# The 18 looped units of a Mamba and token-mixing kernel written out as straight code on every engine

## The reference

```
x = x + mamba(channel_norm(x))        # per batch a sequence of 2304 tokens of 128 channels, plus one token
t = to_tokens(x)                      # 576 tokens of 512 channels
t = t + route(token_norm(t))          # tokens 1..128 are replaced by a weighted sum of 8 of 256 memory blocks
out = from_tokens(t)

def mamba(seq):
    u, z = split(seq @ in_proj)                      # 256 inner channels
    u = silu(conv4(u) + bias)
    dt, B, C = split(u @ x_proj)                     # rank 8, 16 states, 16 states
    dt = softplus(dt @ dt_proj + bias)
    for each token:                                  # a scan over 2305 tokens
        h = exp(dt * A) * h + (dt * u) * B           # 16 states per inner channel
        y = sum(h * C)
    return (y + u * D) * silu(z) @ out_proj
```

## Time and profile before

| | |
|---|---|
| median of 3 runs | 1336.19 us (1335.76 to 1339.44) |
| the profiled execution | 1343.07 us, of which 1341.3 us span |
| VectorE busy | 1211.3 us, 90% |
| TensorE busy (matmul) | 1094.4 us, 82% |
| GpSimd busy | 1089.0 us, 81% |
| ScalarE busy | 779.3 us, 58% |
| mean granted TensorE clock | 0.94 |

### The profile page before, as it was taken

How to read it: one execution, slowest core, us unless ns; L and a number is a source line. 1 busy time by engine, 2 the same in 40 slices (tenths; PEclk the granted TensorE clock), 3 DMA queues, 4 the chain that set the end, 5 groups by cost and what they waited for, 6 DMA issues and landing times.

```text
span 1341.3 us, 16943 instructions
## 1 busy us (share of the span) xinstructions
PE 1094.4 (82%) x3770; PEld 641.5 (48%) x3770; DVE 1211.3 (90%) x1440; ACT 779.3 (58%) x1423; POOL 1089.0 (81%) x699
## 2 busy tenths in 40 slices
PE   6687888887887887877877877977977888877997
PEld 4343454444444544544544534534534544533887
DVE  1499999999999999999999999999999999999761
ACT  2465665666666666666666656656656656656230
POOL 3288799798898888898898898898897998987850
PEclk9688988999989989989989989989989989888999
DMA  6221221222221221221221222212212213214361
GB/s 155 73 96 48 99 85 68 77 96 78 77 96 62 93 96 54 94 101 55 94 88 67 96 69 86 95 55 100 95 55 100 96 55 116 94 56 140 110 179 30
DMA packets 64537, 116.64 MB, mean 87 GB/s; under 512 B 34218, under 2 KB 47954, under 8 KB 64466
## 3 DMA queue, kind: packets, MB, share of 16 engines
q1 hardware_dynamic: 64466, 115.96, 25.4%
HBM read 108.47 MB, written 7.47 MB: 86 GB/s over the span
## 4 chain that ended last, share of the span: by engine, by line
DVE 44%; issue 21%; PE 18%; ACT 11%; DVEq 3%; POOL 2%; DMA 0%; ACTq 0%; POOLq 0%; SPq 0%
DVE SCAN L936 26%; DVE SCAN L887 8%; PE Yp L672 4%; ACT DA L480 4%; DVE GATES L922 3%; PE PP L701 3%; PE PP L751 3%; POOL SCAN L412 2%; PE PP L716 2%; PE PP L784 2%; DVE VV L898 2%; DVE UDT L1015 2%; DVE GATES L1038 1%; ACT GATES L563 1%; DVE X L1022 1%
## 5 line engine op out<-in xcount | busy, mean ns | idle before, releaser
L412 POOL TENSOR_TENSOR SCAN<-SCAN,CS 128x768 f32<-128x768 f32 x384 | 695.1, 1824 | 99.8 <-DVE SCAN L936 94.3
L936 DVE TENSOR_TENSOR_SCAN SCAN<-DA,CAR,SCAN 128x384 f32<-128x384 f32 x768 | 728.5, 995 | 4.6 <-ACT DA L480 4.0
L672 PE MATMUL Yp<-SCAN,IDENT 128*128 128x384 f32 x1536 | 594.9, 513 | 145.5 <-DVE VV L898 75.8
L480 ACT ACTIVATE DA<-UDT,A 128x384 f32<-128x384 f32 x768 | 442.9, 582 | 446.6 <-DVE SCAN L936 443.6
L672 PEld LDWEIGHTS Yp<-SCAN,IDENT 128*128 128x128 f32 x1536 | 288.5, 198 | 352.2 <-issue 139.5
L887 DVE TENSOR_TENSOR SCAN<-UDT,BB 128x768 f32<-128x768 f32 x288 | 269.0, 934 | 26.8 <-PE BB L654 16.1
L420 POOL TENSOR_TENSOR SCAN<-UDT,BS 128x768 f32<-128x768 f32 x96 | 175.5, 1828 | 0.0
L818 PE MATMUL PP<-XN,WT 128*128 (+1 forms) x384 | 141.8, 505 | 0.2
L654 PE MATMUL BB<-PT,SEL 96*128 96x384 bf16 x288 | 96.6, 336 | 20.3 <-DVE SCAN L887 20.3
L436 POOL TENSOR_TENSOR UDT<-UDT 128x768 f32<-128x768 f32 x24 | 43.4, 1809 | 76.4 <-DVE UDT L1042 76.4
L818 PEld LDWEIGHTS PP<-XN,WT 128*128 128x128 f32 x384 | 73.4, 196 | 59.8 <-issue 16.4
(11 more groups left out here) (156 smaller groups left out, 1130.7 us busy)
## 6 DMA issues: line engine op xcount, KB each, us to landing
CS<-bc_rows SPq DMA_DIRECT2D x96, 768.0 KB, 4.0
BS<-bc_rows SPq DMA_DIRECT2D x24, 768.0 KB, 5.9
out<-XN SPq DMA_DIRECT2D x32, 192.0 KB, 2.5
X<-in_x SPq DMA_DIRECT2D x24, 192.0 KB, 3.4
X<-in_L_ffn_memory_tokens SPq DMA_DIRECT2D x16, 256.0 KB, 3.2
XN<-in_L_ffn_memory_tokens SPq DMA_DIRECT2D x16, 256.0 KB, 3.1
bc_rows<-XDT SPq DMA_DIRECT2D x24, 48.0 KB, 1.5
X<-in_L_ffn_memory_router SPq DMA_DIRECT2D x1, 512.0 KB, 3.5
```

What stands on the lines that cost most here:

```text
L412: pool.tensor_tensor(M[:, n1 % MRING], HB[:, n1 % HRING], over_halves(CS[:, n1 % CRING]), ALU.mult).then_inc(m_ready, 1)
L480: act.activation(DA[:, h, 0:T], DT[:, par, h], ACT.Exp, scale=A[:, h, n:n + 1])\
L672: last = pe.matmul(Yp[:, h, 0:T], IDENT[:, :], M[:, n3 % MRING, h], start=n3 == 0, stop=n3 == NS - 1)
L936: dve.tensor_tensor_scan(HB[:, s % HRING, h], DA[:, h, 0:T], HB[:, s % HRING, h], CAR[:, ds(J * NS * HALVES + s * HALVES + h, 1)], ALU.mul ...
```

## The change

Two loops become Python loops, so that the program holds every unit as code of its own, with constant addresses and constant counts. Nothing else is edited.

```diff
@@ -245,7 +245,7 @@
             unit(0, 0, back=False)
             unit(1, 1)
-            with eng.Fori(1, (UNITS - 4) // 2) as i:
+            for i in range(1, (UNITS - 4) // 2):
                 unit(2 * i, 0)
                 unit(2 * i + 1, 1)
             unit(UNITS - 4, 0)
@@ -334,7 +334,7 @@
             spread(0, 0)
-            with sp.Fori(0, CHUNKS - 1) as c:
+            for c in range(CHUNKS - 1):
                 for b in range(BATCH):
                     spread(c * BATCH + b + 1, 1 - b % 2)
                     store(c, b, c * BATCH + b)
```

## The result

The changed kernel takes 1329.41 us (median of 6 runs, 1326.50 to 1331.22), the kernel before on the same chip 1338.05 us (6 runs, 1335.76 to 1342.11). The ratio is 0.993 with an interval of 0.9907 to 0.9952: faster by 8.6 us, inside the range of 1314 to 1333 us, 7.2 us above the predicted time and 1.4 us above the upper end of the forecast's own range (1317 to 1328). The profiled execution took 1329.06 us, span 1327.3. That is the very number the prediction gave for it (1329.1), and we shall see that this is partly luck: before's profiled execution lay 5.0 us above its median, this one lies at its own.

What follows compares the result with a forecast made beforehand. VectorE, and what holds it up for reasons other than work, was taken to set the end. Terms -11.2 - 4.7 + 0.7 + 1.2 = -14.0 us took 1336.2 to 1322.2 us; range 1314 to 1333, forecast's own 1317 to 1328.

Steps and rivals of the forecast that it cites:

- branch back: VectorE idle behind the eight taken branches at the loop's head: straight code removes 1.3 + 0.08 us each, 11.2 us gained.
- register instructions at L918: VectorE's 18 waits at L918 for PE's mean: idle falls from 0.45 to 0.23 us a unit, 4.7 us gained.
- small losses elsewhere in the loop: Register instructions other than those ahead of the mean: nearly all run ahead under queued VectorE work and cost nothing.
- more code to fetch: Instruction fetching in the straight units: an "issue" wait of 0.2 us in one unit of three, 1.2 us lost.
- TensorE's clock: Half clock behind L898 delays BB and DA: 7 of 18 units pay 0.95 us each, net 0.7 us lost.
- rival 3: Idle time at the loop's head is GpSimd's and stays when the branch goes: 1333.4 us, chance 0.05.
- The other engines' branches: Branches of PE, ACT and POOL at the loop's end: costed at nothing, since VectorE ends later than they do.
- Rival 4: Straight code starves a sequencer, 1.36 us of VectorE idle in each unit, 24.5 us added: 1345.5 us, chance 0.05.
- the 2 to 10 us: Sign of a right forecast: VectorE's waits at L936 and L887 for DA and BB total this over the 18 units.
- rival 1: All 18 units pay for TensorE's low clock behind L898, 50.9 us each: 1332.1 us, chance 0.20.
- rival 2: None of the 18 units pays for TensorE's low clock behind L898: 21.8 us gained, 1314.4 us, chance 0.10.
- Leave as it is: Runs' median lies 6.9 us below the profiled execution, put down to clock luck; the 14.0 us saving is applied to it unchanged.

## Why the prediction was right in direction, and where it was off

| step, us over the 18 units | predicted | measured |
|---|---|---|
| branch back | -11.2 | -11.2 in the waits and overlap; -11.3 with the clock out of play |
| register instructions at L918 | -4.7 | -4.5; -4.6 with the clock out of play |
| small losses elsewhere in the loop | 0 | about -2.2, with the clock out of play |
| more code to fetch | +1.2 | +0.7, two places |
| TensorE's clock | +0.7 | +7.4 |
| sum | -14.0 | -9.9 (the second figures add up to -10.0, by rounding) |

*The branch.* Shown. The 8 gaps go when VectorE's stream is straight, whatever the others do; they stay at 10.6 us when it alone is looped; and they are 2 when there are 2 branches. This takes away rival 3. That the row named GpSimd was the wait's carrier and not its cause. The other engines' branches were put at nothing because "VectorE ends later than they do at the loop's end"; this reason does not hold by the rows of the kernel before, where two sequencers branch after VectorE's at 465.6 us:

```profile
L248 ACTq COMPARE_BRANCH  x1: 53/53/53, 467.5 to 467.5; - x1
L248 POOLq COMPARE_BRANCH  x1: 45/45/45, 469.8 to 469.8; - x1
```


Their next instructions come within 0.3 us in rounds of two, and behind VectorE's own gap nothing of them shows. With VectorE alone straight they show as 8 waits of 0.2 us (1.7 in all), and in rounds of six they cost 1.2 us a branch.

*The register instructions.* Shown by the waits at L918, and split: 0.49 us a unit looped, 0.34 with only VectorE straight (6.1 / 18), 0.24 with all straight. Both hops count, VectorE's with 0.15 us and the other engines' with 0.10.

*More code to fetch.* Right in kind, half in size: 0.36 us at L1042 of unit 13 and about 0.35 us at L936 of unit 19. That these two are fetches is inferred: what each waited for by the profile was no later than in other units, and in both places a packet on queue q14 starts 0.7 us behind the delayed instruction. The packets went from 59 and 12 to 43 and 30, two more in all, where I had expected many more; the bytes rose from 0.68 to 0.84 MB. Rival 4, a starving sequencer, needed 24.5.

*The clock.* This term failed, in both of its factors: the share of units that pay, above all, and the price. The step read "I take 7 of 18, as many as wait for DA now": 12 units pay. And the price is 1.10 us (50.95 - 49.85), not 0.95, because a unit that pays nothing is 49.85 us long. Against the kernel without low clock, the changed kernel's 18 units lose 14.0 us (911.6 - 897.6): 13.2 for the twelve, 0.5 for three units at 50.0, 0.35 for the fetch in unit 19. For the kernel before the same loss is 6.2 us (921.5 - 915.3), close to the 5.9 taken. So straight code gained 17.7, the clock took back 7.4 and the pause in unit 19 another 0.35. The waits for DA and BB, 11.1 us, also lie above the 2 to 10 us that were to show the forecast right. The argument against rival 1, that a shifting idle time can't stay in the bad place, was wrong: it stays for three to five units, passes the good place in two, and starts again. Rival 1 was the better picture of two thirds of the units, rival 2 of one third.

*From the profile to the median.* Its own difference of 14.0 came out to the digit, but by two errors that cancel: the 18 units gave 4.1 us less than forecast and the rest of the kernel 4.1 us more. The rest is not the change's. Its code is the same, and the time ahead of unit 2's L898 came out between 165.2 and 168.4 us over all the profiles. Behind unit 20 most of the 1.9 us lies in the 7 waits of L887 for BB. Here is their row from 1088 us to the end of the kernel before, and from 1076 us to the end of the one after:

```profile
DVE SCAN L887 <- PE BB L654: 11.3, 7, 3.9
```

```profile
DVE SCAN L887 <- PE BB L654: 9.6, 7, 3.9
```

The medians, 8.6 us apart, are nearer to the 9.9 of the 18 units. Of the 7.2 us by which the forecast of 1322.2 missed, some 4.1 are the units', 1.9 the new median of the kernel before (1338.05 for 1336.19), and 1.3 lie between those 9.9 and 8.6. "Leave as it is" took it for granted that a saving read from an execution 6.9 us above the median holds at the median; this was not tested. How much each run of either kernel pays for the clock in the 18 units cannot be read from unprofiled runs, and stays open.

## What to carry to other kernels

Look at how long the busiest engine stands idle right behind each branch back, and straighten that engine's stream first: here VectorE's alone brought 12.8 of 17.7 us. Longer rounds mean fewer branches, but each can then hold up engines that it did not before: here 2.5 us a branch instead of 1.3. Before crediting a gain in a kernel whose TensorE rests once in each round, count the rounds with a low granted clock, before and after: here they took back 7.4 us of 17.7. Spare matmuls returned all of it only where they ran inside the idle time and both idle times had them: with VectorE alone straight, late ones turned a ratio of 0.9863 into 0.9995, and in the straight kernel filling one of two idle times moved the low clock to the other.

## What the runs showed of the hardware

- VectorE has nothing to do for 1.2 to 1.5 us behind a taken branch, in every kernel where its stream is looped, whether the other engines' streams are or not. The loops of the other engines together cost 4.9 us over the 18 units with both idle times filled (902.5 against 897.6): 1.9 at the line that was L918, 1.7 in 8 waits of the scans for GpSimd, the rest in small differences over many instructions.
- How long a sequencer takes from its branch back to its next instruction went with the length of its round, and not alike on all engines. With rounds of two units, of 368 recorded instructions on VectorE, 189 on ScalarE and 165 on GpSimd, it was 2.8 us on VectorE and 0.2 to 0.3 us on the other two; with rounds of six, three times as long, 2.8, 3.3 and 2.6 us. On TensorE it went from 0.3 to 3.5 us.
- A pause of 0.36 us stands in unit 13 at the same instruction (L1042) in every kernel whose VectorE stream is straight throughout, and in none where it is looped. In each of them a packet on queue q14 starts 0.66 to 0.69 us behind that instruction's start.
- The low clock of TensorE can be moved. In the changed kernel it lies behind L898; with that time filled it lay 20 us later; with both filled, none was left in the 18 units of the straight kernel, and TensorE's mean granted clock rose from 0.930 to 0.981.
